# A state-space stage with its start, its first units and its tail reordered, and two reordered places in the stage behind it

## The reference

```
proj = x @ in_proj_w.T                        # gate, xBC, dt
xBC  = silu(causal conv of 4 taps over tokens (xBC) + conv_b)
x, B, C = split(xBC)                          # 128 heads of 64; 8 groups of B and C, state 128
dt   = clip(softplus(dt + dt_bias), 0.001, 100)
cs   = cumsum(dt * A) in each chunk of 128 tokens
Y    = ((C.B) * tril(exp(cs_l - cs_s))) @ (x * dt)     # in a chunk, plus the state carried between the two chunks
yg   = (Y + x * D) * silu(gate)
out  = (yg * rsqrt(mean(yg^2 in the group) + eps)) * norm_w @ out_proj_w.T
```

## Time and profile before

| | us |
|---|---|
| median of 3 runs | 2137.88 (2137.70 to 2138.59) |
| profiled execution | 2137.98 |
| its span | 2136.2 |
| stage C begins on PE | 439.1 |
| first units begin on PE | 577 |
| stage D begins on PE | 1942.4 |

### The profile page before, as it was taken

How to read it: one execution, slowest core, us unless ns; L and a number is a source line. 1 busy time by engine, 2 the same in 40 slices (tenths; PEclk the granted TensorE clock), 3 DMA queues, 4 the chain that set the end, 5 groups by cost and what they waited for, 6 DMA issues and landing times. The chain is left out here.

```text
span 2136.2 us, 35778 instructions
## 1 busy us (share of the span) xinstructions
PE 2083.9 (98%) x10641; PEld 1669.7 (78%) x10641; DVE 1672.2 (78%) x2922; ACT 1385.5 (65%) x2744; POOL 672.2 (31%) x416
## 2 busy tenths in 40 slices
PE   9999999989989999999999999999999999998998
PEld 7888778867867787878777777878778777877876
DVE  7655446458888888888888888888888888878875
ACT  3222125433488888879888888888878888863232
POOL 6644334311113324233333324233333323330010
PEclk9999999999999999999999999999999999999999
DMA  5312404222332222232222223232332322212432
GB/s 196 110 56 91 163 1 133 74 51 95 118 138 100 92 101 99 69 124 69 98 95 98 98 84 108 70 113 74 103 113 70 108 85 99 76 48 84 143 98 80
DMA packets 63887, 204.31 MB, mean 96 GB/s; under 512 B 14960, under 2 KB 15216, under 8 KB 55184
## 3 DMA queue, kind: packets, MB, share of 16 engines
q1 hardware_dynamic: 63760, 202.97, 27.7%
HBM read 194.04 MB, written 8.91 MB: 95 GB/s over the span
## 5 line engine op out<-in xcount | busy, mean ns | idle before, releaser
L72 PE MATMUL bank<-xT_hi,C_w_hi 128*128 128x512 f32 x1160 | 474.6, 409 | 6.5 <-POOL C_w_lo L1746 2.5
L73 PE MATMUL bank<-xT_lo,C_w_hi 128*128 128x512 f32 x1160 | 461.8, 398 | 0.0
L74 PE MATMUL bank<-xT_hi,C_w_lo 128*128 128x512 f32 x1160 | 461.1, 398 | 0.0
L1719 POOL TENSOR_TENSOR C_w_lo<-C_raw,C_w_hi 128x512 fp32r<-128x512 f32 x130 | 168.7, 1298 | 862.2 <-ACT C_w_hi L1816 798.8
L1411 DVE SCALAR_TENSOR_TENSOR C_acc<-bank,C_par,C_acc 128x510 f32<-128x510 f32 (+2 forms) x384 | 282.6, 746 | 93.6 <-ACT C_acc L1771 70.3
L1517 DVE TENSOR_TENSOR C_decay<-C_decay,C_cb 128x512 f32<-128x512 f32 x384 | 265.4, 719 | 40.8 <-ACT C_decay L1913 36.3
L72 PEld LDWEIGHTS bank<-xT_hi,C_w_hi 128*128 128x128 f32 x1160 | 219.9, 190 | 64.6 <-issue 11.4
L74 PEld LDWEIGHTS bank<-xT_hi,C_w_lo 128*128 128x128 f32 x1160 | 219.5, 189 | 53.3
L73 PEld LDWEIGHTS bank<-xT_lo,C_w_hi 128*128 128x128 f32 x1160 | 219.8, 190 | 47.0
L72 PE MATMUL bank<-C_out_hi,C_yg_hi 128*128 128x512 f32 x512 | 200.8, 392 | 5.0 <-DVE C_yg_lo L1487 4.7
L74 PE MATMUL bank<-C_out_hi,C_yg_lo 128*128 128x512 f32 x512 | 200.0, 391 | 0.0
(11 more groups left out here) (280 smaller groups left out, 4288.6 us busy)
## 6 DMA issues: line engine op xcount, KB each, us to landing
C_cs_row<-cs_rows SPq DMA_DIRECT2D x64, 1024.0 KB, 5.4
C_raw<-in_Cxg SPq DMA_DIRECT2D x65, 512.0 KB, 3.6
ahead_raw<-in_D SPq DMA_DIRECT2D x32, 512.0 KB, 3.6
C_raw_out<-in_Cout SPq DMA_DIRECT2D x64, 256.0 KB, 2.9
...
```

Source lines behind the costliest of these rows:

```text
L72: pe.matmul(out, lh, rh, start=start, stop=False)
L73: pe.matmul(out, lh, rl, start=False, stop=False)
L74: return pe.matmul(out, ll, rh, start=False, stop=stop)
L1719: e.tensor_tensor(w_lo[:, slot, :], raw_at, f32(w_hi[:, slot, :]), ALU.subtract).then_inc(lo_done, 1)
```

## The change

- Start: PE's second dt product waits for each quarter of the low part of x by itself. On ACT the four taps of i = 0 and 1 stand inside the dt chain. On DVE the memsets of `dt_steps` and half of `bc_conv(0)` come before `bc_high(1)`, the other half before `bc_high(2)`. SP loads group 0's C.B into `cb` during the start, in front of the store of cs.
- Unit 0: the last C.B is moved after both halves of the convolution, into three free rows of `group_out` instead of `decay`, and has a store semaphore of its own (`cb_last`). On ACT x_silu and ease of both halves come ahead of all Exp, and second_exp ahead of gate_silu, as in the other units.
- The two quantised tiles move from unit 1 to units 2 and 3, with another scratch tile; the first output additions into `group_out` wait for them and for `cb_last`.
- POOL does `squares` before `out_low`.
- Tail: 12 dummy matmuls before the last inside; the first `squares_sum` before output tile 0.
- Stage D: in tile 0 of both passes hidden_low comes right behind hidden, ahead of split13. In pass 1, tile 0, PE does the gate product, then `down(0, 15)`, then the up product, and DVE does `half_sum(0)` before hidden.

```diff
@@ -717,9 +717,10 @@
                     if kind == "D":
-                        hidden(hf, n, par)
                         if hf and isinstance(n, int) and n == 0:
                             half_sum(0)
+                        hidden(hf, n, par)
+                        if isinstance(n, int) and n == 0:
                             hidden_low(hf, n, par)
@@ -732,7 +733,7 @@
                         hidden(hf, n, par)
-                    elif not (hf and isinstance(n, int) and n == 0):
+                    elif not (isinstance(n, int) and n == 0):
                         hidden_low(hf, n, par)
@@ -1024,12 +1025,13 @@
-            def gate_up(hf, n, par):
+            def gate_up(hf, n, par, parts=(0, 1)):
                 slot = (hf * TL + par) % 2
 ...
                     pe.wait_ge(hid_done, n + (hf * TL - 1))
-                for i, done in ((0, gate_mm), (1, up_mm)):
+                for i in parts:
+                    done = (gate_mm, up_mm)[i]
                     out = sh.bank[4 + 2 * slot + i][:, :]
@@ -1121,7 +1123,12 @@
                         pe.wait_ge(fold2_done, n + 1)
-                    if not (kind == "D" and hf == 0 and isinstance(n, int) and n == 0):
+                    if kind == "D" and isinstance(n, int) and n == 0:
+                        if hf:
+                            gate_up(hf, n, par, (0,))
+                            down(0, TL - 1, (TL - 1) % 2, False, True)
+                            gate_up(hf, n, par, (1,))
+                    else:
                         gate_up(hf, n, par)
@@ -1139,8 +1146,6 @@
                         down(hf, n - 1, 1 - par, isinstance(n, int) and n == 1, False)
-                    elif kind == "D" and hf:
-                        down(0, TL - 1, (TL - 1) % 2, False, True)
                     if turns and late:
@@ -1280,7 +1285,7 @@
-            cb_stored0 cb_stored1 cb_in raw_in0 ...
+            cb_stored0 cb_stored1 cb_last cb_in raw_in0 ...
@@ -1289,8 +1294,10 @@
-        def products(pe, out, w_slot, h):
+        def products(pe, out, w_slot, h, ready=None):
             for k in range(KT):
+                if ready is not None:
+                    pe.wait_ge(ready, k + 1)
                 c = slice(P * k, P * (k + 1))
@@ -1302,6 +1309,12 @@
             return slice(HALF * h, HALF * (h + 1))
+
+        def cb_place(g):
+
+            if g == GROUPS - 1:
+                return group_out[:, 2:5, :]
+            return decay[:, 3 * (g % 2):3 * (g % 2) + 3, :]
@@ -1338,11 +1351,13 @@
                 sp.wait_ge(S.cb_moved, 5 * g + 5)
-                sp.dma_start(cb_rows[g, :, :], decay[:, 3 * (g % 2):3 * (g % 2) + 3, :].rearrange("p a t -> p (a t)"))\
-                  .then_inc(cb_stored[g % 2], 16)
+                sp.dma_start(cb_rows[g, :, :], cb_place(g).rearrange("p a t -> p (a t)"))\
+                  .then_inc(cb_stored[g % 2] if g < GROUPS - 1 else S.cb_last, 16)
 ...
                 if g == 4:
+                    sp.wait_ge(S.cb_stored0, 16)
+                    sp.dma_start(cb[:, :, :].rearrange("p a t -> p (a t)"), cb_rows[0, :, :]).then_inc(S.cb_in, 16)
                     sp.wait_ge(S.dt_chain_v, DT_V)
@@ -1376,9 +1391,6 @@
             def load_cb(u):
-                if u.first:
-                    sp.wait_ge(S.cb_stored0, 8 * GROUPS)
-                    sp.wait_ge(S.cb_stored1, 8 * GROUPS)
                 wait(sp, S.m_done, u.U * ROUNDS)
@@ -1391,7 +1403,10 @@
                     store_cb(GROUPS - 1)
-                if u.group_first:
+                if u.first_pair and u.j == 1:
+                    sp.wait_ge(S.cb_stored0, 8 * GROUPS)
+                    sp.wait_ge(S.cb_last, 16)
+                if u.group_first and not u.first:
                     load_cb(u)
@@ -1422,18 +1437,22 @@
-            def bc_conv(i):
+            def bc_conv(i, halves=(0, 1)):
                 g, s = i // 2, i % 2
                 w = lambda n: raw_bc[:, g % 2, 2 * D + (TAPS + 1) * s + n:2 * D + (TAPS + 1) * s + n + 1]
-                for h in range(2):
+                for h in halves:
                     v.wait_ge(S.bc_tap, 2 * i + h + 1)
 ...
             def move_cb(g):
-                e = decay[:, 3 * (g % 2):3 * (g % 2) + 3, :]
+                e = cb_place(g)
                 v.wait_ge(S.cb_mm, 2 * g + 1)
-                wait(v, cb_stored[g % 2], 16 * (g // 2))
+                if g < GROUPS - 1:
+                    wait(v, cb_stored[g % 2], 16 * (g // 2))
+                else:
+                    v.wait_ge(S.dt_chain_v, DT_V)
+                    v.wait_ge(S.dt_moved, 5)
                 for bp in range(2):
@@ -1450,6 +1469,7 @@
                 v.memset(reset[:, 0:N:CHUNK], 0.0).then_inc(S.dt_chain_v, 1)
+                yield
                 v.wait_ge(S.dt_chain_a, 5)
@@ -1502,6 +1522,8 @@
                         v.wait_ge(S.dt_chain_v, DT_V)
+                        v.wait_ge(S.cb_last, 16)
+                        v.wait_ge(ahead.w13_ready, u.j + 1)
                     elif u.j == 0:
@@ -1523,7 +1545,7 @@
                         v.wait_ge(S.cb_stored0, 8 * GROUPS)
-                        v.wait_ge(S.cb_stored1, 8 * GROUPS)
+                        v.wait_ge(S.cb_stored1, 8 * (GROUPS - 2))
                 for b in range(BATCH):
@@ -1580,11 +1602,14 @@
             dt_next = dt_steps()
+            next(dt_next)
+            bc_conv(0, (0,))
             bc_high(1)
+            bc_conv(0, (1,))
+            bc_high(2)
             for i in range(2 * GROUPS):
-                if i == 0:
-                    bc_high(2)
-                bc_conv(i)
+                if i:
+                    bc_conv(i)
                 if 0 < i < 2 * GROUPS - 2:
@@ -1614,13 +1639,13 @@
                 for i in range(2):
-                    v.tensor_scalar(dtz[:, D * i:D * (i + 1)], ahead.raw13[:, n, D * i:D * (i + 1)],
+                    v.tensor_scalar(quarters[3][:, D * i:D * (i + 1)], ahead.raw13[:, n, D * i:D * (i + 1)],
                                     ahead.thr[:, i:i + 1], 1.0, ALU.is_gt, ALU.subtract).then_inc(ahead.above_done, 1)
 ...
                                                  in0=ahead.raw13[:, n, D * i:D * (i + 1)], scalar=ahead.nthr[:, i:i + 1],
-                                                 in1=dtz[:, D * i:D * (i + 1)], op0=ALU.is_ge, op1=ALU.add)
+                                                 in1=quarters[3][:, D * i:D * (i + 1)], op0=ALU.is_ge, op1=ALU.add)
                 ins.then_inc(ahead.w13_ready, 1)
@@ -1631,12 +1656,12 @@
                 for h in range(2):
-                    if u.first and h == 1:
-                        move_cb(GROUPS - 1)
                     v.wait_ge(S.tap, U * 2 + (h + 1))
 ...
                         conv(v, bank[h], lambda n: par_of(U, n), acc[:, :], h, i, S.conv, U * 6)
-                if not u.first:
+                if u.first:
+                    move_cb(GROUPS - 1)
+                else:
                     for h in range(2):
@@ -1645,9 +1670,8 @@
                 clamp(u, 1)
-                if u.first_pair and u.j == 1:
-                    quantised(0)
-                    quantised(1)
+                if isinstance(g, int) and u.adds_first:
+                    quantised(u.j)
                 if u.group_ended:
@@ -1754,11 +1778,11 @@
                 low(S.g_w_hi, 1, raw[:, 1 - s, D:2 * D], S.g_w_lo, U + 2)
+                if not u.first:
+                    squares(u)
                 if u.j == 1:
 ...
                     out_low(U, 1)
-                if not u.first:
-                    squares(u)
                 if u.group_left:
@@ -1793,12 +1817,15 @@
                 a.activation(dtz[:, half(h)], bank[4 + h][:, :], ACT.Identity, bias=dt_bias).then_inc(S.dt_chain_a, 1)
+                bc_tap(0, h)
             a.wait_ge(S.dt_chain_a, 2)
 ...
             a.activation(dte, dta, ACT.Exp, scale=-1.0).then_inc(S.dt_chain_a, 1)
+            bc_tap(1, 0)
             a.wait_ge(S.dt_chain_a, 4)
             a.activation(dte, dte, ACT.Ln, bias=1.0).then_inc(S.dt_chain_a, 1)
+            bc_tap(1, 1)
             def chunk_ends():
@@ -1828,10 +1855,12 @@
                     x_weights(0, 0)
-                bc_tap(i, 0)
+                if i > 1:
+                    bc_tap(i, 0)
                 if i:
                     bc_silu(i - 1, 1)
-                bc_tap(i, 1)
+                if i > 1:
+                    bc_tap(i, 1)
                 bc_silu(i, 0)
@@ -1892,7 +1921,7 @@
                 if u.first:
-                    a.wait_ge((S.cb_stored0, S.cb_stored1)[h], 8 * GROUPS)
+                    a.wait_ge((S.cb_stored0, S.cb_stored1)[h], 8 * (GROUPS - 2 * h))
                 for b in range(BATCH):
@@ -1901,8 +1930,6 @@
                 for h in range(2):
-                    if u.first and h == 1:
-                        ease(u, 1)
                     for b in range(BATCH):
@@ -1942,22 +1969,17 @@
                 ease(u, 0)
+                x_silu(u, 1)
+                ease(u, 1)
                 if not u.first:
```

(16 more changed lines are left out.)

2 lines of the change are left out of this document (1 added, 1 removed).

## The result

| | before | changed |
|---|---|---|
| median, us | 2137.79 (2136.70 to 2138.59, 4 runs) | 2119.67 (2118.26 to 2121.77, 4 runs) |
| ratio | | 0.9917, 95% interval 0.9902 to 0.9932 |
| profiled execution, us | 2137.98 | 2118.26, span 2116.5 |

So it is faster by 0.7 to 1.0%; 2119 was forecast. First the page's table of busy time of the changed kernel, which answers to the earlier trace rows.

What follows compares the result with a forecast made beforehand. TensorE, busy 98% of the span, was taken as the bound, so only its idle and half-clock time could be won. 7.3 + 4.3 - 0.3 + 4.2 + 0.1 + 3.3 = 18.9 us off 2138.0 gave 2119 us, range 2113 to 2127.

Steps and rivals of the forecast that it cites:

- Step 1: Start of the state-space stage: second C.B blocks start 7.3 us earlier, and the lead is kept whole.
- Step 2: Units 0 and 1: out_tile(2,0) starts earlier, 4.3 us taken, range 3.3 to 5.0.
- Step 3: Quantised tiles in units 2 and 3: a loss of 0.3 us, from 0 to 1; GpSimd's squares ahead of out_low cost zero.
- Step 4: Tail: earlier mean square gains 5.8 us, less 1.6 for one half-clock stretch; 4.2 us, range 3.0 to 5.8.
- Step 5: Last stage, first pass: down(0,0) starts earlier but VectorE's chain gives the lead back; 0.1 us, from -1.7 to 4.0.
- Step 6: Last stage, second pass: shorter PE wait and no half-clock stretch behind it; 3.3 us, range 1.6 to 3.7.
- B: Rival, four places with new waits: half-clock stretches follow them, all at once 5.0 us less gain, 2124 us; chance 0.22.
- C: Rival, last stage's first pass or tail: PE's lead survives or clock stays full, 3 to 4 us more, 2115; chance 0.11.
- D: Rival, loop of 62 units: it settles later, PE waits at each out_tile, slower, 2156 us; chance 0.03.
- E: Rival, whole kernel: waits move to the next place and nothing is left, 2138 us; chance 0.04.
- F: Rival, unit 1: table switches cost more than their row shows, 1.36 us more gain for each of two, 2116; chance 0.02.

Runs made afterwards that it cites:

- e2: Only the edits around units 0 to 3, put onto the kernel before: median 2131.42 us, ratio 0.9976.
- e5: Changed kernel with the last stage's first pass in its old VectorE order (hidden_low of tile 0 behind the weight split): 2119.61 us, ratio 0.9919.
- e12: The changed kernel run again with not one character different: 2120.60 us, ratio 0.9923.
- e10: Changed kernel with the first C.B load issued late again, behind the last group's store and the wait for all stores: 2127.75 us, ratio 0.9964.
- e7: Changed kernel with both quantised tiles back in unit 1: 2118.47 us, ratio 0.9905.
- e3: Only the tail's edits (12 dummy matmuls, squares before out_low, earlier first squares_sum), put onto the kernel before: 2131.93 us, ratio 0.9979.
- e9: e8 plus ScalarE's two copies of output weights of units 0 and 1 moved behind the taps: 2113.30 us, ratio 0.9886 to the kernel before.
- e6: Changed kernel without the 12 filler matmuls ahead of the last unit: 2120.81 us, ratio 0.9918.
- e4: Only the last stage's edits, put onto the kernel before: 2134.54 us, ratio 0.9983.
- e8: Changed kernel with VectorE's two dt operations one conv block later and ScalarE's chunk ends at i = 6: 2116.31 us, ratio 0.9894.

## Why the prediction was right, point by point

- **Step 1, 7.3; 6.7 measured.** The new wait (1.23 us, predicted 1.6) and the old one (2.85, predicted 2.3) are where they were put, and half clock follows the second and not the first. The missing 0.6 us is one term: two dt operations of DVE, 1.9 us in my replay, took 2.7. The second was 0.69 in the kernel before, with POOL idle (timeline of DVE, kernel before):

```profile
478.69 0.69 DVE L1457 TENSOR_SCALAR C_sq_sum<-C_sq_sum 128x1024 f32<-128x1024 f32 x1
```
  In the changed kernel it lies beside POOL's low part of the weights, and both are longer (DVE, then POOL, changed kernel):

```profile
471.92 1.47 DVE L1477 TENSOR_SCALAR C_sq_sum<-C_sq_sum 128x1024 f32<-128x1024 f32 x1
```
```profile
463.48 1.09 POOL L1743 TENSOR_TENSOR C_w_lo<-ahead_first,C_w_hi 128x512 fp32r<-128x512 f32 x1 [2.45 <-DVE C_w_hi L1438]
470.83 2.00 POOL L1743 TENSOR_TENSOR C_w_lo<-ahead_first,C_w_hi 128x512 fp32r<-128x512 f32 x1 [6.26 <-DVE C_w_hi L1438]
```
  The Trainium skill, "SBUF — State Buffer", section Who interferes with whom, has such pairs take an exclusive lock, so that the later one stands still for all of the other. These rows agree: DVE's operation ends at 473.39, which is POOL's end, 472.83, and 0.56 more, close to its 0.69 alone. I moved DVE's work in time and did not ask what POOL does beside it. From here to the second C.B blocks the work starts 0.6 to 0.8 us later than in the replay, the 0.7 us of the start-up taken off.
- **Step 2, 4.3, with 5.0 for a full clock.** 5.4 in the profiled execution at a full clock; 3.8 in e2, 3.8 in e5 and 2.6 in e12 with half clock at out_tile(2,0). So 4.3, a mean of the two cases, stands for the median, though no single execution shows it, and the traces run past both ends of the range of 3.3 to 5.0: the replay was too slow by some 0.4 us at full clock, and a stretch of 6.8 us was not among its cases. Both new waits came (1.55 for 1.85; 3.14 for 1.5 to 3.1). The mechanism was told unevenly: I priced the load of C.B by DVE's 2.81 us of waiting. e10 shows that more hangs on it: with the last C.B moved behind the convolution and the load behind its store, inside(1) is 6.7 us later, and from the last C.B blocks later than in the kernel before. Which share the order of ScalarE's work has by itself stays open.
- **Step 3, -0.3; 0.** No PE wait and no loss to unit 4. e7 shows that its purpose in time is small: without it out_tile(2,0) is 2.3 us late in one trace, and the median does not see it.
- **Step 4, 4.2; 3.7.** The first column sums in the wait, out tile 0 behind them and the chain of 11.4 us behind the mean square came as told; one half-clock stretch too. In the traces without a stretch (e3, e7, e9) the tail gains 5.2 to 5.3 us, where I had 5.8, so the 0.5 us too much lie in the replay and not in the clock. New is a wait of 1.24 us for C_out_lo, where I had 0.9 for y_low; step 3 had charged nothing for POOL's squares ahead of out_low, and in the tail PE does wait for it (timeline of POOL, changed kernel):

```profile
1895.91 2.81 POOL L1760 TENSOR_TENSOR C_sq_sum<-C_sq_sum,C_sg 128x1024 f32<-128x1024 f32 x1 [0.63 <-DVE C_decay L1539]
1898.68 3.39 POOL L1751 TENSOR_TENSOR C_out_lo<-C_raw_out,C_out_hi 128x512 fp32r<-128x512 f32 x2
```
  Of the filler I said that it keeps the clock. At its place it does, in nine traces of nine; e6 shows that the time hardly gains by it, since a stretch a few us later comes in its stead.
- **Step 5, 0.1; 0.1**, and shown by e5: down(0,0) 2.2 us earlier, given back before the transposes. I looked for it at the transposes' own wait, 0.63 before. It is 0.42 in the three traces that have a stretch on the way (changed kernel, e7, e9) and 1.26 to 1.29 in the six that have none (e4, e6, e8, e10 to e12), so it does grow, though not to the 1.5 that I gave; more of the lead goes into the new wait of 1.84 us before down(0,1).
- **Step 6, 3.3; 3.0.** Wait 0.33 for 0.4, no half clock, in e4 as well. Beside POOL's additions hidden_low takes 1.55 us, where I had 1.3, and ends 0.4 us behind the last of them (2025.54); the 128 columns behind it (kept_l) take 0.28 us and meet POOL no more, so it was hidden_low that waited for the fourth addition and not kept_l.
- **Rivals.** B was half there: the stretch behind 3.14 us is in six of seven traces, and costs 1.4 to 2.8, which can be why the medians are 2119.6 to 2120.8 and not 2118; the executions behind the medians have no trace. C is out by e5. D is out: the loop gained 0.8 us. E is out by the result, and each of the four parts alone is faster than the kernel before. F was not tried by itself; a table load takes 1.28 us in the changed kernel too, and with F the full-clock lead of step 2 would have been 7.7 and not 5.4.

That the sum came within 0.8 us of the profiled execution is partly luck: steps 2 and 3 gave 1.4 more than forecast and the group changes 0.8, the end 0.6; steps 1, 4 and 6 gave 1.4 less and the start-up took 0.7.
